# Finding the rows of each expert's blocks: a table written by scatter, against one-hot matmuls and gathers in the loop

## The reference

```python
x = L0_attn_x
xn = _layernorm(x, axis=-1)
x = x + _L0_attn_ref(xn, ...) + _L0_ffn_ref(xn, ...)
# attention
q = (x @ Wq + bq).reshape(B, S, H, Dh)
latent = x @ Wl + bl
k = (latent @ Wk + bk).reshape(B, S, H, Dh)
v = (latent @ Wv + bv).reshape(B, S, H, Dh)
attn = softmax(einsum('bihd,bjhd->bhij', q, k) * SCALE)
out = einsum('bhij,bjhd->bihd', attn, v).reshape(B, S, D) @ Wo + bo
# experts
logits = xt @ Wg.T + bg
top_vals, top_idx = jax.lax.top_k(logits, TOPK)
rw = softmax(top_vals)
gate, up = (xt @ Wgu[e] + bgu[e]) split into even and odd columns
gate = minimum(gate, 7.0); up = clip(up, -7.0, 7.0)
out_e = ((up + 1.0) * gate * sigmoid(gate * 1.702)) @ Wd[e] + bd[e]
out = sum over the two chosen experts of rw * out_e
```

## Time and profile before

| | |
|---|---|
| median of 3 runs | 464.88 us (464.76 to 465.46) |
| the profiled execution, its own time | 465.35 us |
| its span in the trace | 463.6 us |
| TensorE matmul busy | 437.4 us (94%) |
| VectorE busy | 379.9 us (82%) |
| ScalarE busy | 309.3 us (67%) |
| GpSimd busy | 204.0 us (44%) |
| granted TensorE clock, mean | 0.947 |

### The profile page before, as it was taken

How to read it: one execution, slowest core, us unless ns; L and a number is a source line. 1 busy time by engine, 2 the same in 40 slices (tenths; PEclk the granted TensorE clock), 3 DMA queues, 4 the chain that set the end, 5 groups by cost and what they waited for, 6 DMA issues and landing times.

```text
span 463.6 us, 9089 instructions
## 1 busy us (share of the span) xinstructions
PE 437.4 (94%) x2681; PEld 205.5 (44%) x2681; DVE 379.9 (82%) x757; ACT 309.3 (67%) x356; POOL 204.0 (44%) x238
## 2 busy tenths in 40 slices
PE   0998999999999999999999999999999999999995
PEld 0455444344444444454444454444444443333453
DVE  7569998989898998888898989898989899985112
ACT  1524004588878787787778777878787877677861
POOL 7042767415172636552454447244636274950000
PEclk9978555999999999999999999999999999999997
DMA  5995681362523233321514150504100413300001
GB/s 146 174 161 179 139 196 52 94 195 68 145 52 105 76 76 60 114 76 46 78 59 123 34 101 24 165 24 82 28 6 6 74 18 85 101 2 1 24 24 45
DMA packets 38275, 37.79 MB, mean 82 GB/s; under 512 B 5664, under 2 KB 33414, under 8 KB 37800
## 3 DMA queue, kind: packets, MB, share of 16 engines
q1 hardware_dynamic: 34320, 32.52, 30.7%
q0 software_dynamic: 2944, 4.75, 3.9%
q10 hardware_dynamic: 984, 0.20, 0.2%
HBM read 23.51 MB, written 13.67 MB: 80 GB/s over the span
## 4 chain that ended last, share of the span: by engine, by line
PE 62%; DVE 22%; ACT 8%; issue 5%; DMA 1%; DVEq 0%; ACTq 0%; SPq 0%
PE banks L1013 18%; DVE half_max L833 18%; PE banks L996 15%; PE banks L1065 12%; ACT probs L698 5%; PE banks L1084 3%; PE banks L1086 2%; PE banks L1021 2%; PE banks L931 1%; ACT th L690 1%; PE banks L955 1%; PE banks L1049 1%; DMA y<-in_x 1%; PE banks L924 1%; ACT pv_sb L671 1%
## 5 line engine op out<-in xcount | busy, mean ns | idle before, releaser
L833 DVE TENSOR_REDUCE half_max<-banks 128x1 f32<-128x512 f32 x512 | 321.6, 683 | 33.3 <-PE banks L996 32.6
L698 ACT ACTIVATE probs<-banks 128x1024 f32<-128x1024 f32 x256 | 254.3, 1024 | 112.7 <-PE banks L1065 109.0
L996 PE MATMUL banks<-k_rows,q_rows 62*128 62x512 f32 x512 | 181.9, 468 | 4.1 <-DVE half_max L833 2.4
L1065 PE MATMUL banks<-q_rows,k_rows 64*128 64x512 f32 x512 | 143.4, 456 | 2.5 <-ACT probs L698 1.9
L1013 PE MATMUL banks<-probs,v_pad 128*32 128x512 f32 x1024 | 137.2, 608 | 0.1
L996 PEld LDWEIGHTS banks<-k_rows,q_rows 62*128 62x128 f32 x512 | 82.6, 196 | 91.5 <-DVE half_max L833 78.5
L1065 PEld LDWEIGHTS banks<-q_rows,k_rows 64*128 64x128 f32 x512 | 57.4, 187 | 69.4 <-ACT probs L698 58.9
L580 POOL DMA_INDIRECT moe_table<-x_rows,result_row x48 | 47.9, 998 | 61.5 <-ACT x_rows L686 44.0
L550 POOL TENSOR_TENSOR gate<-gate,w_blk 128x512 f32<-128x512 f32 x12 | 12.5, 1044 | 77.1 <-ACT gate L682 77.1
L540 POOL DMA_INDIRECT x_table<-xn,place_u x32 | 31.2, 976 | 21.1 <-DVE place_u L814 11.6
L1013 PEld LDWEIGHTS banks<-probs,v_pad 128*32 128x32 f32 x1024 | 20.2, 108 | 42.1 <-issue 29.9
(11 more groups left out here) (119 smaller groups left out, 305.3 us busy)
## 6 DMA issues: line engine op xcount, KB each, us to landing
w_blk<-in_wexp SPq DMA_DIRECT2D x48, 193.0 KB, 3.0
q_rows<-q_parts SPq DMA_DIRECT2D x56, 64.0 KB
k_rows<-k_parts SPq DMA_DIRECT2D x56, 64.0 KB
x_table<-blank SPq DMA_DIRECT2D x1, 3096.0 KB, 21.5
x_rows<-x_table SPq DMA_DIRECT2D x12, 258.0 KB, 3.6
q_parts<-q SPq DMA_DIRECT2D x8, 256.0 KB
k_parts<-k SPq DMA_DIRECT2D x8, 256.0 KB
y<-in_x SPq DMA_DIRECT2D x4, 256.0 KB, 4.4
```

The source lines that it names most:

```text
L698: nc.scalar.activation(probs[:, (2 * s + part) % 4, :, :], banks[:, bank:bank + 2, :], ACT.Exp, scale=SCALE).then_inc(slot_free, 1)
L833: nc.vector.tensor_reduce(half_max[:, unit, row, half:half + 1], banks[:, ring_bank(job), :], AX_X, ALU.max).then_inc(ring_free, 1)
L996: pe.matmul(bank, q_rows[slot][rows, half, pair, P * qb:P * qb + P], k_rows[slot][rows, pair, 512 * keys:512 * keys + 512], start=True, st ...
L1065: mm = pe.matmul(banks[:, bank + u, :], k_rows[(unit // 2) % 2][rows, pair, P * kb:P * kb + P], q_rows[(unit // 2) % 2][rows, half, pair, ...
```

## The change

The scatter of the tokens and `x_table` go. SyncE stores the normalised rows in order into `tokens` (line 389 of the new kernel). A group's rows are gathered into SBUF by GpSimd with 4 indirect transfers (`gather`), of which the first three groups come before the loop and nine within it, at pairs 6, 10, 14 and, one turn on, 3. For that the token of each place is needed. It is found by matmuls: for each of the 32 sets of 128 chosen pairs one matrix of 128 by 128 marks the row within a block (`at_row`), another of 128 by 96 holds, for the 48 blocks, the set's number and the token's row where the token is in that block (`token_in`). The 32 products are added up in bank 2 (`find_tokens`), ScalarE copies them out, and GpSimd turns them into row numbers.

The places, block numbers and expert numbers are computed by GpSimd and no longer by VectorE, from a copy of the counts that ScalarE makes. VectorE keeps three small steps at the 19th of the 48 jobs, and does the weights' three at the 9th. The one-hot matrices are made by GpSimd (the first 16 `at_row`, `in_block`, one half of `token_in`) and ScalarE (the other 16 `at_row` by a square and a ReLU, the other half of `token_in`).

```diff
--- before.py
+++ after.py
@@ -50,7 +49,7 @@
 WEIGHTS_IN = {HEAD: -2, 5: -1, 11: 0, 13: 1}
-ROWS_IN = {4: -2, 6: -1, 12: 0, 15: 1}
+GATHER = {3: -2, 6: -1, 10: 0, 14: 1}
...
@@ -144,9 +143,7 @@
-
-    x_table = nc.dram_tensor("x_table", (BLOCKS * P, XW), F32, kind="Internal").ap()
+    tokens = nc.dram_tensor("tokens", (B * S, D), F32, kind="Internal").ap()
...
@@ -370,18 +385,14 @@
 
-            sp.wait_ge(s_blank, 2)
-            sp.dma_start(x_table.rearrange("(n p) d -> p n d", p=P), blank[:, None, :].to_broadcast([P, BLOCKS, XW])).then_inc(s_cleared, 16)
+            sp.wait_ge(s_xn, TILES)
+            sp.dma_start(tokens.rearrange("(t p) d -> p t d", p=P), xn[:, :, :]).then_inc(s_tokens, 16)
...
-            def load_rows(m):
-                i = m % SLOTS
-                sp.dma_start(x_rows[:, i, :, :], x_by_group[m]).then_inc(s_xrows[i], 16)
...
@@ -466,14 +469,14 @@
                             load_back(h)
-                    for places, bring in ((WEIGHTS_IN, weights_in), (ROWS_IN, rows_in)):
-                        m = SLOTS * (t + 1) + places.get(p, GROUPS)
-                        if SLOTS <= m < GROUPS:
-                            bring(m)
+                    m = SLOTS * (t + 1) + WEIGHTS_IN.get(p, GROUPS)
+                    if SLOTS <= m < GROUPS:
+                        weights_in(m)
...
@@ -519,25 +516,79 @@
             first_k_rows(pool)
-            pool.wait_ge(s_place, 1)
-            pool.wait_ge(s_cleared, 16)
-            for n in range(2 * TILES):
...
-                pool.indirect_dma_start(x_table, bass.IndirectOffsetOnAxis(place_u[:, k, t:t + 1], 0), xn[:, t, :], None).then_inc(s_scattered, 16)
+            def add_up(total, terms):
+                for w in (8, 4, 2):
+                    link(nc.gpsimd.tensor_tensor(terms[:, :, 0:w], terms[:, :, 0:w], terms[:, :, w:2 * w], ALU.add))
+                return nc.gpsimd.tensor_tensor(total, terms[:, :, 0], terms[:, :, 1], ALU.add)
+            pool.wait_ge(s_counted, 1)
+            iota_e = iota_b[:, 0:NEXP]
+            link(nc.gpsimd.tensor_scalar(full[:], counted[:, TILES, :], 1.0 / P, 1.0, ALU.mult, ALU.mult))
+            link(nc.gpsimd.tensor_tensor(over[:, :, :], full[:].unsqueeze(2).to_broadcast([P, NEXP, NEXP]),
+                                         iota_e[:, None, :].to_broadcast([P, NEXP, NEXP]), ALU.subtract))
+            link(nc.gpsimd.tensor_scalar(over[:, :, :], over[:, :, :], 0.0, 1.0, ALU.is_gt, ALU.mult))
+            link(add_up(blocks_of[:], over))
+            link(nc.gpsimd.tensor_tensor(over[:, :, :], lower[:, :, :], blocks_of[:, None, :].to_broadcast([P, NEXP, NEXP]), ALU.mult))
+            link(add_up(first_block[:], over))
+            link(nc.gpsimd.tensor_scalar(first_row[:], first_block[:], float(P), 1.0, ALU.mult, ALU.mult))
+            link(nc.gpsimd.tensor_tensor(place[:, :, :], counted[:, 0:TILES, :], first_row[:, None, :].to_broadcast([P, TILES, NEXP]), ALU.add))
+            for k, hot in ((0, hot1), (1, hot2)):
+                link(nc.gpsimd.tensor_tensor(place_k[:, k, :, :], hot[:, :, :], place[:, :, :], ALU.mult))
+            add_up(place_f[:, :, :].rearrange("p k t -> p (k t)"), place_k[:, :, :, :].rearrange("p k t e -> p (k t) e")).then_inc(s_place_f, 1)
+            link(nc.gpsimd.tensor_tensor(end_block[:], first_block[:], blocks_of[:], ALU.add))
+            link(nc.gpsimd.tensor_scalar(ended[:], end_block[0:BLOCKS, :], iota_b[0:BLOCKS, P:P + 1], 1.0, ALU.is_le, ALU.mult))
+            link(add_up(expert_f[:], ended[:, None, :]))
+            link(nc.gpsimd.tensor_scalar(expert_f[:], expert_f[:], float(NEXP - 1), 1.0, ALU.min, ALU.mult))
+            nc.gpsimd.tensor_copy(expert_i[:], expert_f[:]).then_inc(s_expert, 1)
+            pool.wait_ge(s_place, 3)
+            for i in range(2):
+                nc.gpsimd.tensor_copy(place_n[:, i, :], place_at[:, i, :]).then_inc(s_place_n, 1)
+            pool.wait_ge(s_place_n, 2)
+            link(nc.gpsimd.tensor_tensor(in_block[:, :, :], place_n[:, 1, :].unsqueeze(2).to_broadcast([P, 2 * TILES, BLOCKS]),
+                                         iota_b[:, None, 0:BLOCKS].to_broadcast([P, 2 * TILES, BLOCKS]), ALU.subtract))
+            nc.gpsimd.tensor_scalar(in_block[:, :, :], in_block[:, :, :], 0.0, 1.0, ALU.is_equal, ALU.mult).then_inc(s_hot, 1)
+            pool.wait_ge(s_hot, 1)
+            nc.gpsimd.tensor_tensor(token_in[:, :, :, 0, :].rearrange("p k t b -> p (k t) b"), in_block[:, :, :],
+                                    iota_b[:, P + 1:P + 1 + 2 * TILES].unsqueeze(2).to_broadcast([P, 2 * TILES, BLOCKS]), ALU.mult).then_inc(s_hot, 1)
+            for t in range(TILES):
+                last = nc.gpsimd.tensor_scalar(at_row[:, 0, t, :], iota_b[:, 0:P], place_n[:, 0, t:t + 1], 1.0, ALU.is_equal, ALU.mult)
+            last.then_inc(s_hot, 1)
+            pool.wait_ge(s_v, CHUNKS)
+            fill_v(0, 0)
+            fill_v(1, 1)
+            pool.wait_ge(s_weighed, 1)
+            for k, hot in ((0, hot1), (1, hot2)):
+                link(nc.gpsimd.tensor_tensor(hot[:, :, :], hot[:, :, :],
+                                             tw[:, 2 + k, :].unsqueeze(2).to_broadcast([P, TILES, NEXP]), ALU.mult))
+            nc.gpsimd.tensor_tensor(cw[:, :, :], hot1[:, :, :], hot2[:, :, :], ALU.add).then_inc(s_cw, 1)
+            pool.wait_ge(s_cw, 1)
+            pool.wait_ge(s_ids, 1)
+            link(nc.gpsimd.tensor_scalar(result_n[:], fetched[:, 0, :], float(P), -float(P), ALU.mult, ALU.add))
+            link(nc.gpsimd.tensor_tensor(result_n[:], result_n[:], fetched[:, 1, :], ALU.add))
+            link(nc.gpsimd.tensor_scalar(token_n[:], result_n[:], float(B * S), -float(B * S), ALU.is_ge, ALU.mult))
+            link(nc.gpsimd.tensor_tensor(token_n[:], token_n[:], result_n[:], ALU.add))
+            link(nc.gpsimd.tensor_scalar(token_n[:], token_n[:], 0.0, 1.0, ALU.max, ALU.mult))
+            link(nc.gpsimd.tensor_copy(token_u[:], token_n[:]))
+            link(nc.gpsimd.tensor_scalar(empty_n[:], fetched[:, 0, :], 0.0, 4.0 * B * S, ALU.is_equal, ALU.mult))
+            link(nc.gpsimd.tensor_tensor(empty_n[:], empty_n[:], result_n[:], ALU.add))
+            link(nc.gpsimd.tensor_copy(result_u[:], empty_n[:]))
+            def gather(m):
+                i = m % SLOTS
+                if m >= SLOTS:
+                    pool.wait_ge(s_res_out[i], 16 * GB * (m // SLOTS))
+                for q in range(GB):
+                    pool.indirect_dma_start(x_rows[:, i, q, :], None, tokens,
+                                            bass.IndirectOffsetOnAxis(token_u[:, GB * m + q:GB * m + q + 1], 0)).then_inc(s_xrows[i], 16)
+            pool.wait_ge(s_tokens, 16)
+            gather(0)
...
@@ -568,17 +619,10 @@
 
-            def rows_of(m):
-                i = m % SLOTS
-                pool.wait_ge(s_xrows[i], 16 * (m // SLOTS + 1))
-                nc.gpsimd.tensor_copy(result_row[:, i, :], x_rows[:, i, :, D]).then_inc(s_row, 1)
-                pool.wait_ge(s_row, m + 1)
...
-                pool.indirect_dma_start(moe_table, bass.IndirectOffsetOnAxis(result_row[:, i, q:q + 1], 0),
-                                        x_rows[:, i, q, 0:D], None,
+                pool.indirect_dma_start(moe_table, bass.IndirectOffsetOnAxis(result_u[:, GB * m + q:GB * m + q + 1], 0),
+                                        x_rows[:, i, q, :], None,
...
@@ -592,6 +636,11 @@
             def pair(t, p, last):
+                m = SLOTS * (t + 1) + GATHER.get(p, GROUPS)
+                if p == 1 and t == 0:
+                    gather(1)
+                if m < GROUPS:
+                    gather(m)
...
@@ -659,6 +707,8 @@
             nc.scalar.activation(tw[:, 1, :], tw[:, 0, :], ACT.Exp).then_inc(s_egap, 1)
+            act.wait_ge(s_rank, 1)
+            nc.scalar.activation(counted[:, :, :].rearrange("p t e -> p (t e)"), banks[:, RANK_BANK, 0:(TILES + 1) * NEXP], ACT.Copy).then_inc(s_counted, 1)
...
@@ -710,7 +760,19 @@
+
+            act.wait_ge(s_place_n, 2)
+            for t in range(TILES):
+                nc.scalar.activation(at_row[:, 1, t, :], iota_b[:, 0:P], ACT.Square, scale=-1.0,
+                                     bias=place_n[:, 0, TILES + t:TILES + t + 1]).then_inc(s_square, 1)
+            act.wait_ge(s_square, TILES)
+            nc.scalar.activation(at_row[:, 1, :, :], at_row[:, 1, :, :], ACT.Relu, scale=-1.0, bias=1.0).then_inc(s_at_row, 1)
+            act.wait_ge(s_hot, 1)
+            nc.scalar.activation(token_in[:, :, :, 1, :].rearrange("p k t b -> p (k t) b"), in_block[:, :, :], ACT.Copy,
+                                 scale=iota_b[:, P:P + 1]).then_inc(s_rowed, 1)
             move_max(act, 0, TURN_OF_FIRST)
+            act.wait_ge(s_ids_ps, 1)
+            nc.scalar.activation(fetched[:, :, :].rearrange("p w b -> p (w b)"), banks[:, IDS_BANK, 0:2 * BLOCKS], ACT.Copy).then_inc(s_ids, 1)
...
@@ -796,34 +858,6 @@
 
-            dve.wait_ge(s_rank, 1)
```

(39 more changed lines are left out.)

94 lines of the change are left out of this document (33 added, 61 removed).

## The result

The changed kernel takes **476.19 us** (median of 3 runs, 476.03 to 476.27) against 464.88: ratio 1.0239, 95% interval 1.0216 to 1.0263. It is slower, as forecast, but by 11.3 us and not by 2.5, and it lies above the range, which ended at 470.8.

The account below looks back on a forecast made before the run. VectorE was taken to set the pace until 71.3 us, then TensorE's half clock in the first pair. Terms summed to +3.3 us at the start of the pairs, 2.5 kept: 467.4 us against 464.88, range 464.3 to 470.8.

Parts of the forecast that it names:

- term 4: Last eight jobs before the pairs: four one-hot matmuls ahead of each cost +1.9 us (0.8 to 4.1); GpSimd's comparisons just hidden.
- terms 2 and 3: VectorE's jobs: weights' steps at the ninth +0.57, places' steps at the nineteenth +0.45, waits for GpSimd's step in flight +0.7.
- term 3: VectorE's products at the ninth and 32nd jobs wait for GpSimd's step in flight: +0.7 us (0.1 to 2.2).
- rival C: GpSimd's one-hot work is late, TensorE waits 2 us at the 45th job: 470.0 us, chance 0.11.
- Term 1: VectorE's first reduction comes sooner, less ScalarE's new copy of the counts: net -0.5 us (-0.9 to -0.3).
- Terms 5 and 6: Copy of token numbers before the first scores +0.2 us, early gathers hidden; the loop's gathers hidden by 0.5 us, 0.
- Rival D: In the loop, gathers make tanh late in four places by about 1 us each: 471.4 us, chance 0.11.
- Term 7: First pair: the clock rises at about its old time, so a delay of 3.3 costs 3.3 x 0.75 = 2.5 us.

Follow-up runs that it names:

- act_rows: The changed kernel with GpSimd's 16 `at_row` matrices made by ScalarE too, so ScalarE makes all 32: 469.56 us, ratio 1.0094.
- Act_double: As act_rows, but each of the 32 one-hot matmuls issued twice, the second into a bank nobody reads: 470.71 us, ratio 1.0131.
- act_paired: As act_rows, but the 32 one-hot matmuls in four sets of eight, ahead of every second job: 468.69 us, ratio 1.0078.
- find_spread: As act_rows, but `at_row` in four parts, first transfer of the maxima on SyncE's queue, matmuls spread over more jobs: 465.69 us, ratio 1.0020.
- experts_pool: The kernel before with only the steps from block ends to expert numbers moved to GpSimd: 462.16 us, ratio 0.9942, on the first chip.
- weights_later: As experts_pool, but VectorE's three steps for the weights at its 8th job: 480.11 us, ratio 1.0032, on the second chip.

## Why the prediction was wrong

It had the stretch and the sign right. Two sizes were wrong, one of them turned a wait that was held to be hidden into 5.1 us, and what was to come back by the clock didn't. From the forecast's +3.3 at the start of the pairs to the 12.0 measured: +5.1 the wait, +2.5 term 4, +1.6 the front (1.1 later in this profile where 0.5 sooner was forecast), -0.9 terms 2 and 3, +0.4 the rest.

**The step that failed** is in term 4: "GpSimd's 16 small comparisons (0.29 for 128 columns) end at 66 to 69; they are needed at 69.6. Just hidden." The 0.29 is the row of a cast; a comparison with a multiplication takes 0.69. The long comparison, in term 3 taken "as 0.614 for 512", takes three times that rate, 5.40. So the matrices came at 78.7, and act_rows shows that this alone was 5.2 us. It is rival C, which had a chance of 0.11 and a price of 2 us of waiting; its 470.0 was too low as well. It should have been priced by the bounds: no row showed a comparison by GpSimd, and I let the nearest rows stand as if they had no upper end. The chance should have been larger than a tenth for a need with 0.6 us to spare. The Trainium skill, in GPSIMD Engine Reference, section "7. Performance pitfalls for Q7 kernels", gives 2.03 cycles for a comparison body that isn't unrolled against 1.03 for one that is. The ratio measured here is 3.2 (1.96 against 0.62), and (max, mult), which compares nothing, has it too, so the page's figures do not explain these rows.

**Term 4's own size**: +1.9 with bounds 0.8 to 4.1, measured 4.4, above the upper bound. The one-hot matmuls were 0.08 each where 0.09 was taken. A job by itself takes 0.835 in its step, where 0.48 was taken and 0.55 was the bound, from the eleven matmuls of the earlier trace rows which still ran side by side. Act_double and act_paired show both. With groups of four and six ahead of pairs of jobs, as in find_spread, the stretch from TensorE's being free for the 37th job to the first scores is 74.10 - 64.95 = 9.15, less the wait of 1.06 is 8.09, against 71.32 - 64.86 = 6.46 before: the 32 matmuls cost 1.6 us, near the 1.9.

**Term 1**, -0.5: 0.8 at the same clock (act_rows). That only 0.9 us of VectorE's work was late, "the point of the whole case", is right: in experts_pool 0.2 us at most is left to win there, in weights_later nothing. But the front moves by 2 us between traces, which is more than the term.

**Terms 2 and 3**, together +1.7: 0.8 from the first reduction to the 37th job. The places were hidden as said: GpSimd's sums ended at 49.8, used at 55.5. GpSimd's step in flight held VectorE up by 0.2 at the weights' first step (0.38 us in place of 0.17; in act_rows it was the third, the product, with 0.48) and by nothing at the unit's end, where the product began as GpSimd's long comparison was ending (64.72, 64.77).

**Terms 5 and 6** hold on the first chip. Turns are 96.8 us, as before; gathers are 1.25 apart, the landing of the scatters was awaited for 1.54 us; the gate was clipped at 160.3 and tanh began at 160.86, by the forecast 0.5 us of slack. Rival D did not come. On the other chips the loop is where most of the loss lies, and no term had that.

**Term 7**, the factor of 0.75, is wrong for this kernel: the clock rose 12.0 us later, with the first pair and not at its old time, and nothing came back by it but 0.2 us. It isn't wrong in itself: its condition, a rise "at about the same time", came true in find_spread, where the first scores were 2.8 us late, the rise was at 79.4, and about half of the delay was back at the first group's rows. In act_double the first scores came 2.2 us after act_rows' and the rise 0.7 us sooner. Both have less idle time on TensorE ahead of the scores (1.1 us and none, where the changed kernel has 5.1); that this decides is not shown.

## What to carry to other kernels

Before work goes to an engine with much free time, price each instruction by a row of the very same pair of operations: on GpSimd the neighbour pair can cost three times as much. If the result has a date, compare that date with the worst price, and give matrices to the engine that makes them by cheap steps (here ScalarE). Half-height matmuls that run side by side stay next to each other, with the full-height ones in groups between such pairs; and if an engine's work is late by less than another engine's own finish, only that difference can be won.

## What was not expected of the hardware

- GpSimd's two-operation steps: 0.61 to 0.62 us for 512 columns with (mult, add), (add, mult), (min, max); 1.92 to 2.03 with (is_equal, mult), (is_gt, mult), (is_equal, add), (is_equal, max), (max, mult), (max, min), (add, max). With 128 columns and a number for each partition 0.72 for (is_equal, mult) and for (max, mult).
- At half clock a single half-height job between full-height matmuls takes 0.835 us, and two next to each other, on the upper and the lower half, take 0.84 together.
- One program's front has TensorE's clock at a half for 7 or for 10 us, and the first job comes 1.5 (43.17 and 41.63) or 2.2 us apart (41.04 and 43.22); the two traces are of different chips each time.
- A delay of 2.8 us ahead of the pairs left the rise of the clock where it was (79.4, find_spread), one of 12.0 moved it by 12.0.
- The same kernel takes 465.0 us on one chip and 478.7 and 478.9 on two others, and a change's ratio was 1.024 on the first and 1.075 on the second.
